# A new order of the work ahead of the steady loop in a metaformer kernel on one core

## Chip, core and metric

The kernel runs on one core of one Trainium2 chip. The metric is device time in microseconds of one execution, taken as the median of several runs. The engines are named as in the profile: PE is TensorE, DVE is VectorE, ACT is ScalarE, POOL is GpSimd, and SP is SyncE, which here only issues DMAs. An SBUF tensor is one in the on-chip working memory; PSUM is the memory that PE writes.

## What is computed

The input x has 16 images of 512 channels and 24 x 8 positions. The reference is, cut to its core:

```python
# attention, over xn = (x - mean_c) / sqrt(var_c + 1e-6), statistics over the channels
ca = sigmoid(mlp(mean_hw(xn)) + mlp(max_hw(xn)))     # mlp(v) = relu(v @ fc1_w.T) @ fc2_w.T, 512 -> 64 -> 512
xa = xn * ca
s  = conv7x7(concat(mean_c(xa), max_c(xa)), sa_w)    # two planes to one, padding 3
x  = x + xa * sigmoid(s)
# feed-forward, per token of 512 channels
def bitlinear(v, w):
    rms = rsqrt(max(mean(w * w), 1e-5))
    wq  = clip(round(w * rms), -1, 1) / rms
    sc  = 127 / max(max(abs(v)), 1e-5)
    return (clip(round(v * sc), -128, 127) / sc) @ wq.T
t = tokens(x)                                         # 16 * 192 tokens
t = t + bitlinear(gelu(bitlinear(layernorm(t), w1)), w2)   # w1: 2048 x 512, w2: 512 x 2048
```

So each weight needs the mean of its squares over the whole matrix before any of it can be rounded, and each image needs its channel gate before the convolution, and the convolution before its feed-forward part.

## The kernel before

The 16 images are taken as 8 pairs of 2 images. A pair has 384 tokens, which are 3 tiles of 128. Everything is written by hand: each engine has one list of instructions, and semaphores tie the lists together. The order in the text of an engine's block is the order in which that engine executes; there is no scheduler, and an instruction that waits holds up all that stands behind it on its engine.

A pair goes through these stages. `load_x` brings it in; `turn_x` on PE turns each tile so that tokens lie on the partitions, and `copy_x` on ACT takes it out of PSUM into `xt`. `channel_stats` and `aggregate` (together `stats1`) on DVE make mean and variance, and `normalise1` on POOL makes the normalised rows `v1`, with three small instructions ahead of three large ones. `turn_v1` on PE turns them back in four blocks of 128 channels; for each block DVE takes maxima (`token_max`) and ACT means (`token_mean`). Then `fc1`, `hidden`, `fc2`, `gate_channels` (a tanh), `split_gate` (five small DVE instructions that split the gate into three bfloat16 parts), `turn_ca`, `copy_caT`, `spread_ca`, `scale_channels` (DVE, writes `pv` and the channel maximum), `sum_channels` (ACT), `split_stats`, and `conv` on PE, 42 small matmuls. After `sum_conv`, `gate_tokens` and `token_gate` each tile gets `add_attention`, `centre` (which on the way needs `rs2`, made by `rstd2` on POOL), `round_x` on POOL, `turn_xq`, `copy_xq`, and `ffn_in`: four blocks of four matmuls (L1139), each followed by a GELU on ACT. `hidden_max` and `hidden_scale` on DVE, `round_g` on POOL and `pack_g` on ACT quantise the hidden rows; SP transposes them by DMA, `ffn_out` (L1150) multiplies by w2, `add_ffn` adds the residual, and the result is turned back and stored.

The weights are loaded as four quarters each of 128 x 2048 values (1 MB). `squares` sums the squares of a quarter, on ACT or on DVE (L865); `weight_sum`, `weight_mean` (PE) and `weight_floor` (DVE, L875, writes `w_ms`) lead to `weight_rms` on POOL (L412). Rounding is one multiply-add on a quarter in place: in this kernel DVE does quarters 0 and 2 (L882) and POOL quarters 1 and 3 (L419). `turn_weights` on PE turns them in eight blocks per weight, through the two PSUM banks `ps_t`, and `copy_weights` on ACT (one instruction) or DVE (two) clips them and writes them into `w1T` or `w2T`. The bands are the convolution's matrices: SP loads the taps in eight small DMAs, `make_taps` (DVE), `place_bands` (PE) and `make_bands` (DVE) prepare them.

In the steady loop (`body`, once per pair) the feed-forward part of one pair, the attention part of the second pair after it and the loading of the third overlap. Ahead of the loop stands a prologue that brings pair 0 through attention, tiles 0 and 1 of it through the first half of the feed-forward part, pair 1 through its convolution and pair 2 to its statistics, and that prepares all weights. The change is to the prologue alone.

## Time and profile before

| | us |
|---|---|
| median of 3 runs (321.93 to 323.15) | 323.08 |
| profiled execution, whole | 323.44 |
| profiled execution, span | 321.7 |
| PE busy | 276.9 (86%) |
| DVE busy | 251.6 (78%) |
| ACT busy | 217.7 (68%) |
| POOL busy | 160.9 (50%) |
| HBM read, written | 14.94 MB, 6.29 MB |

Busy times are sums over the span of 321.7 us of one profiled execution; the whole time of that execution is 1.74 us longer. The page cuts the span into 40 slices of 8 us; the prologue is about the first ten of them. Starts are in microseconds from the start of the span. A merged row of a timeline, such as one with x3, covers several instructions of one kind, and its duration is from the first start to the last end.

### The profile page before, as it was taken

Reading aid. Unit: us, or ns where it says so; the run is one execution under the profiler, and the core shown is the slowest. Engines: PE = TensorE matmul, PEld = TensorE weight load, DVE = VectorE, ACT = ScalarE, POOL = GpSimd, SP = SyncE. Lnnn points to the kernel's source line nnn. Section 1 sums busy time; section 2 is a strip of 40 time slices with the busy share of each in tenths; the row PEclk is TensorE's granted clock in tenths of the full one; section 3 lists DMA queues with packets and bytes.
Section 4 is the critical chain, followed back from the end, with each engine's and each line's share of the span. In section 5 each row is a group of like instructions: output and inputs, shape, how many; then the busy total and the mean of one; then the engine's idle time right before and its main releaser. Section 6 shows DMA issues by size and latency. Waiting matters only on the chain.

```text
span 321.7 us, 5840 instructions
## 1 busy us (share of the span) xinstructions
PE 276.9 (86%) x1834; PEld 155.9 (48%) x1834; DVE 251.6 (78%) x590; ACT 217.7 (68%) x442; POOL 160.9 (50%) x256
## 2 busy tenths in 40 slices
PE   2657669596999979997999799979997999999974
PEld 2444644563456445644564456445644453544431
DVE  0757979879698879887988798878897888899510
ACT  2286397568476976697669766876687669677731
POOL 7404355315855475547554755475547553565420
PEclk9999999859699999999999999999999999999999
DMA  5899300002073209320942094219411732063393
GB/s 131 317 387 421 117 1 2 0 0 51 18 166 65 54 15 254 75 50 17 241 89 48 18 238 91 44 25 235 94 36 32 164 68 51 16 163 74 70 218 98
DMA packets 71078, 34.20 MB, mean 106 GB/s; under 512 B 52040, under 2 KB 68424, under 8 KB 70536
## 3 DMA queue, kind: packets, MB, share of 16 engines
q1 hardware_dynamic: 69384, 32.78, 39.6%
q10 hardware_dynamic: 1664, 1.05, 1.2%
q8 instruction: 15, 0.25, 0.3%
q14 instruction: 15, 0.12, 0.1%
HBM read 14.94 MB, written 6.29 MB: 66 GB/s over the span
## 4 chain that ended last, share of the span: by engine, by line
PE 50%; DVE 12%; POOL 12%; ACT 12%; issue 9%; DMA 3%; SPq 1%; ACTq 0%; POOLq 0%; DVEq 0%
PE ps_o L1150 16%; PE ps_h L1139 9%; PE ps_t L1139 8%; POOL w_room L474 4%; POOL v L451 4%; PE front L1072 4%; ACT w_raw L520 3%; ACT junk_p L520 3%; PE front L1062 3%; PE ps_t L1181 2%; PE small L1088 2%; ACT junk L520 2%; DVE w_room L882 2%; POOL rs L445 2%; PE front L1159 1%
## 5 line engine op out<-in xcount | busy, mean ns | idle before, releaser
L1150 PE MATMUL ps_o<-w2T,hq 128*128 128x512 f16 x384 | 92.7, 380 | 1.2 <-DMA hq<-w_raw 1.2
L474 POOL TENSOR_SCALAR w_room<-w_room,q 128x1024 f32<-128x1024 f32 x48 | 59.3, 1247 | 63.8 <-DVE q L849 63.8
L839 DVE TENSOR_REDUCE amax<-w_room 128x1 f32<-128x1024 f32 (+1 forms) x48 | 57.1, 1208 | 2.2 <-ACT w_room L520 2.2
L1139 PE MATMUL ps_h<-w1T,xq 128*128 128x512 f16 x208 | 54.6, 408 | 0.9 <-ACT xq L520 0.9
L1150 PEld LDWEIGHTS ps_o<-w2T,hq 128*128 128x128 f16 x384 | 35.3, 98 | 37.4 <-issue 3.6
L520 ACT ACTIVATE w_raw<-w_room 128x1024 f16<-128x1024 f16 x48 | 49.4, 1049 | 0.6 <-POOL w_room L474 0.6
L520 ACT ACTIVATE w_room<-ps_h,s 128x512 f32<-128x512 f32 x52 | 35.0, 689 | 14.3 <-PE ps_h L1139 13.1
L1139 PE MATMUL ps_t<-w1T,xq 128*128 128x512 f16 x176 | 43.1, 383 | 0.0
L520 ACT ACTIVATE w_room<-ps_t,s 128x512 f32<-128x512 f32 x44 | 30.2, 688 | 8.3 <-PE ps_t L1139 8.3
L520 ACT ACTIVATE junk_m<-front 128x192 bf16<-128x192 f32 x64 | 20.5, 328 | 21.6 <-DVE pooled L754 21.6
L1139 PEld LDWEIGHTS ps_h<-w1T,xq 128*128 128x128 f16 x208 | 19.8, 103 | 24.2 <-issue 4.8
L463 POOL TENSOR_SCALAR cen<-cen,q 128x512 f32<-128x512 f32 x24 | 16.6, 691 | 27.2 <-DVE q L831 27.2
L856 DVE SCALAR_TENSOR_TENSOR res<-ps_o,s,t 128x512 f32<-128x512 f32 x24 | 17.8, 741 | 12.6 <-PE ps_o L1150 12.6
L1072 PE MATMUL front<-id,v 128*128 128x128 f32 x96 | 18.4, 314 | 10.2 <-POOL v L451 7.5
L1139 PEld LDWEIGHTS ps_t<-w1T,xq 128*128 128x128 f16 x176 | 16.9, 99 | 20.7 <-issue 1.3
L1062 PE MATMUL front<-id,x_in 128*128 128x128 f32 x96 | 17.6, 321 | 6.7 <-DMA x_in<-in_x 5.9
L812 DVE SCALAR_TENSOR_TENSOR t<-pv,sg,xt 128x512 f32<-128x512 f32 x24 | 21.2, 885 | 0.3
L1072 PEld LDWEIGHTS front<-id,v 128*128 128x128 f32 x96 | 12.7, 160 | 17.8 <-POOL v L451 9.5
L741 DVE BATCH_NORM_STATS2 st<-xt 128x6 f32<-128x512 f32 x24 | 15.6, 681 | 7.0 <-ACT xt L520 7.0
L451 POOL TENSOR_SCALAR v<-xt,minus_mean,rs 128x512 f32<-128x512 f32 x24 | 19.8, 828 | 1.4
L520 ACT ACTIVATE w_room<-front 128x512 f32<-128x512 f32 x24 | 14.1, 586 | 8.8 <-PE front L1159 8.8
L754 DVE TENSOR_REDUCE pooled<-front 128x2 f32<-128x384 f32 x32 | 17.5, 548 | 2.3 <-PE front L1072 2.1
(125 smaller groups left out, 459.3 us busy)
## 6 DMA issues: line engine op xcount, KB each, us to landing
out<-w_room SPq DMA_DIRECT2D x16, 384.0 KB, 3.2
x_in<-in_x SPq DMA_DIRECT2D x14, 384.0 KB, 5.1
w_room<-in_L_ffn_w SPq DMA_DIRECT2D x4, 1024.0 KB, 9.1
w_raw<-in_L_ffn_w SPq DMA_DIRECT2D x4, 1024.0 KB, 12.3
x_in<-in_x ACTq DMA_DIRECT2D x2, 384.0 KB, 3.9
hq<-w_raw SPq DMA_TRANSPOSE x48, 3.2
fc_raw<-in_L_conv_fc_w ACTq DMA_DIRECT2D x2, 128.0 KB, 4.3
taps_rev<-in_L_conv_sa_w SPq DMA_DIRECT2D x2, 0.2 KB
```

Of the source, the lines that this page charges most:

```text
L451: pool.tensor_scalar(v1[:, s, :], xt[pair.par][:, s, :], minus_mean[:, s:s + 1], rs1[:, s:s + 1], ALU.add, ALU.mult).then_inc(normed, 1)
L463: pool.tensor_scalar(c[:, :], c[:, :], q1[tile.par][:, 0:1], MAGIC, ALU.mult, ALU.add).then_inc(cen_rounded, 1)
L474: pool.tensor_scalar(part, part, q2[tile.par][:, 0:1], MAGIC, ALU.mult, ALU.add).then_inc(g_rounded, 1)
L520: act.activation(out_ap, in_ap, func, **more).then_inc(signal, 1)
L754: dve.tensor_reduce(pooled[:, k, 0:2], front[bank][:, 0:TOK].rearrange("p (i t) -> p i t", i=2), AX.X, ALU.max).then_inc(max_ready, 1)
L812: link(dve.scalar_tensor_tensor(t_tile, pv[par][:, s, :], sg[par][:, s:s + 1], xt[par][:, s, :], ALU.mult, ALU.add))
L839: chain.mark(dve.tensor_reduce(amax2[:, i:i + 1], w1_room[:, first + i * F // 2:first + (i + 1) * F // 2 + i], AX.X, ALU.max, apply_absolu ...
L856: dve.scalar_tensor_tensor(res[tile.par][:, :], ps_o[:, :], s2[tile.third][:, 0:1], t[tile.pair.par][:, tile.s, :], ALU.mult, ALU.add).the ...
L1062: last = pe.transpose(front[bank][:, tile_cols(k)], x_in[tile.pair.par][:, k, tile_cols(tile.s)], id32[:, :])
L1072: last = pe.transpose(front[bank][:, tile_cols(s)], v1[:, s, tile_cols(k)], id32[:, :])
L1139: last = pe.matmul(banks[b], xq[tile.pair.par][:, tile.s, k, :], w1T[:, k, b * 512:(b + 1) * 512], start=(k == 0), stop=(k == NC - 1))
L1150: last = pe.matmul(ps_o[:, :], hq[tile.par][:, k, :], w2T[:, k, :], start=(k == 0), stop=(k == NF - 1))
```

## The change

The instructions that the steady loop issues stay as they are. Ahead of it, five things are written anew.

SP issues the four DMAs of w1 before it waits for the taps' buffer and before the eight tap DMAs, and loads pair 1 between the second and the third quarter of w2 instead of ahead of w2. POOL alone rounds both weights, quarters 0 to 3 of w1 in a row, and of w2 one quarter after tile 0, one after tile 1, two after pair 1's `normalise1`; DVE keeps only the reciprocals (`weight_unit`). Squares are taken differently: DVE does quarters 0 and 1 of both weights, ACT quarters 2 and 3. DVE copies one more block of w1 (block 5). The third part of the bands goes through PSUM bank `ps_t0` rather than `small`, and PE waits for `band_ready` before the first block of w1. And the lists of all four compute engines bring tile 0, then tile 1, of pair 0 into the feed-forward part before pair 1 gets its statistics and its maxima, where before the two were interleaved.

The core of the diff follows. From ACT's list on, and for DVE's and PE's lists, only the new order is shown, and a + marks a line that stands elsewhere or not at all in before.

```diff
-                    small[:, 256:256 + (BAND_ROWS - 2 * PER_BANK) * ROW_COLS])]
+                    ps_t[0][:, :].bitcast(f32)[:, 0:(BAND_ROWS - 2 * PER_BANK) * ROW_COLS])]
...
-        SQUARES_BY_VECTOR = [(2,), (2, 3)]
-        BY_VECTOR = [(1, 3), (1, 5)]
+        SQUARES_BY_SCALAR = (2, 3)
+        BY_VECTOR = [(1, 3, 5), (1, 5)]
...
+            w1_v = w1.rearrange("(k p) c -> p k c", p=P)
+            w2_v = w2.rearrange("(k p) f -> p k f", p=P)
+            for i in range(4):
+                sp.dma_start(w1_raw[:, 4 * i:4 * i + 4, :], w1_v[:, 4 * i:4 * i + 4, :]).then_inc(w1_loaded[i], 16)
...
             for i in range(4):
-                sp.dma_start(w1_raw[:, 4 * i:4 * i + 4, :], w1_v[:, 4 * i:4 * i + 4, :]).then_inc(w1_loaded[i], 16)
-            load_x(Pair(1))
-            for i in range(4):
+                if i == 2:
+                    load_x(Pair(1))
                 sp.dma_start(w2_raw[:, i, :], w2_v[:, i, :]).then_inc(w2_loaded[i], 16)
             load_x(Pair(2))
...
+            def round_weights(k, raw, quarters):
 
                 pool.wait_ge(w_rms_ready, k + 1)
-                for i in (1, 3):
+                for i in quarters:
                     part = quarter(k, raw, i)
-                    pool.tensor_scalar(part, part, w_rms[:, k:k + 1], MAGIC, ALU.mult, ALU.add).then_inc(w_odd_rounded, 1)
+                    pool.tensor_scalar(part, part, w_rms[:, k:k + 1], MAGIC, ALU.mult, ALU.add).then_inc(w_rounded, 1)
...
             weight_rms(0)
-            round_weights(0, w1_raw)
-            normalise1(Pair(1), 0, 1, 2)
+            round_weights(0, w1_raw, (0, 1, 2, 3))
             rstd2(Tile(Pair(0), 0))
             round_x(Tile(Pair(0), 0))
             weight_rms(1)
-            round_weights(1, w2_raw)
+            round_weights(1, w2_raw, (0,))
             rstd2(Tile(Pair(0), 1))
             round_x(Tile(Pair(0), 1))
+            round_weights(1, w2_raw, (1,))
+            normalise1(Pair(1), 0, 1, 2)
+            round_weights(1, w2_raw, (2, 3))
             round_g(Tile(Pair(0), 0))
             rstd2(Tile(Pair(0), 2))
             round_x(Tile(Pair(0), 2))
...
+            squares(0, w1_raw, w1_loaded, 2)
             for k in range(NC):
                 token_mean(pair0, k, k % 2)
+            squares(0, w1_raw, w1_loaded, 3)
             gate_channels(pair0)
             copy_caT(pair0)
+            squares(1, w2_raw, w2_loaded, 2)
             for s in range(NT):
                 sum_channels(Tile(pair0, s))
+            act.wait_ge(masks_ready, 2)
+            copy_weights(0, (0,))
+            copy_x(Tile(pair1, 0), 1)
+            copy_x(Tile(pair1, 1), 0)
+            copy_weights(0, (2,))
+            gate_tokens(pair0)
+            copy_x(Tile(pair1, 2), 1)
+            squares(1, w2_raw, w2_loaded, 3)
+            copy_weights(0, (4,))
+            copy_xq(Tile(pair0, 0), 0)
+            copy_weights(0, (6, 7))
+            gelu(Tile(pair0, 0), None, h_start)
+            copy_weights(1, (0,))
+            copy_xq(Tile(pair0, 1), 0)
+            gelu(Tile(pair0, 1), None, h_start, (0, 1))
+            copy_weights(1, (2,))
+            gelu(Tile(pair0, 1), None, h_start, (2, 3))
+            token_mean(pair1, 0, 1)
+            copy_weights(1, (3,))
+            token_mean(pair1, 1, 0)
+            copy_weights(1, (4,))
+            token_mean(pair1, 2, 1)
+            copy_xq(Tile(pair0, 2), 0)
+            token_mean(pair1, 3, 1)
+            copy_weights(1, (6, 7))
+            pack_g(Tile(pair0, 0))
+            gate_channels(pair1)
+            copy_x(Tile(pair2, 0), 0)
+            copy_x(Tile(pair2, 1), 1)
+            copy_caT(pair1)
             for s in range(NT):
+                sum_channels(Tile(pair1, s))
             copy_x(Tile(pair2, 2), 0)
...
-            def round_weights(k, raw):
+            def weight_unit(k):
 
                 dve.wait_ge(w_rms_ready, k + 1)
-                for i in (0, 2):
-                    part = quarter(k, raw, i)
-                    dve.tensor_scalar(part, part, w_rms[:, k:k + 1], MAGIC, ALU.mult, ALU.add).then_inc(w_even_rounded, 1)
                 if k == 1:
...
             stats1(pair0, 0, 1, 2)
+            squares(0, w1_raw, w1_loaded, (0, 1))
+            token_max(pair0, 0, 0)
+            token_max(pair0, 1, 1)
             make_taps()
+            token_max(pair0, 2, 0)
+            token_max(pair0, 3, 1)
+            hidden(pair0)
+            weight_sum(0)
             make_bands()
+            weight_floor(0)
             split_gate(pair0)
+            squares(1, w2_raw, w2_loaded, (0,))
+            for s in range(NT):
+                scale_channels(Tile(pair0, s), s % 2)
+            weight_unit(0)
+            copy_weights(0, (1,))
             split_stats(pair0)
+            squares(1, w2_raw, w2_loaded, (1,))
             sum_conv(pair0)
             copy_weights(0, (3,))
             token_gate(pair0)
             add_attention(Tile(pair0, 0))
+            weight_sum(1)
             centre(Tile(pair0, 0))
             weight_floor(1)
+            copy_weights(0, (5,))
             add_attention(Tile(pair0, 1))
+            centre(Tile(pair0, 1))
+            weight_unit(1)
+            stats1(pair1, 0, 1, 2)
             dve.wait_ge(w_turned, 8)
             for i in range(2):
                 dve.memset(g_eps[i], EPS).then_inc(eps_ready, 1)
+            hidden_max(Tile(pair0, 0), 0)
+            copy_weights(1, (1,))
+            hidden_max(Tile(pair0, 0), 1)
+            hidden_scale(Tile(pair0, 0))
+            add_attention(Tile(pair0, 2))
+            token_max(pair1, 0, 1)
+            centre(Tile(pair0, 2))
+            token_max(pair1, 1, 0)
+            hidden_max(Tile(pair0, 1), 0)
+            token_max(pair1, 2, 1)
+            hidden_max(Tile(pair0, 1), 1)
+            hidden_scale(Tile(pair0, 1))
+            copy_weights(1, (5,))
             token_max(pair1, 3, 1)
             hidden(pair1)
             split_gate(pair1)
+            channel_stats(pair2, 0, 1)
+            for s in range(NT):
+                scale_channels(Tile(pair1, s), (1, 0, 1)[s])
             split_stats(pair1)
+            channel_stats(pair2, 2)
             sum_conv(pair1)
             aggregate(pair2, 0, 1, 2)
...
+            a = turn_v1(pair0, 0, 0, a)
             b = turn_v1(pair0, 1, 1, b)
             a = turn_v1(pair0, 2, 0, a)
             b = turn_v1(pair0, 3, 1, b)
+            place_bands()
             fc1(pair0)
             fc2(pair0)
+            weight_mean(0)
             turn_ca(pair0)
             a = spread_ca(Tile(pair0, 0), 0, a)
             b = spread_ca(Tile(pair0, 1), 1, b)
+            pe.wait_ge(band_ready, 2)
+            turn_weights(0, w1_raw, (0,))
             a = spread_ca(Tile(pair0, 2), 0, a)
+            turn_weights(0, w1_raw, (1,))
             b = turn_x(Tile(pair1, 0), 1, b)
             a = turn_x(Tile(pair1, 1), 0, a)
+            conv(pair0)
+            turn_weights(0, w1_raw, (2, 3))
             b = turn_x(Tile(pair1, 2), 1, b)
+            turn_weights(0, w1_raw, (4, 5))
+            weight_mean(1)
+            a = turn_xq(Tile(pair0, 0), 0, a)
+            turn_weights(0, w1_raw, (6, 7))
             weights_ready(0)
+            ffn_in(Tile(pair0, 0), h_start)
+            turn_weights(1, w2_raw, (0, 1))
+            a = turn_xq(Tile(pair0, 1), 0, a)
+            ffn_in(Tile(pair0, 1), h_start, (0, 1))
+            turn_weights(1, w2_raw, (2,))
+            ffn_in(Tile(pair0, 1), h_start, (2, 3))
             b = turn_v1(pair1, 0, 1, b)
+            turn_weights(1, w2_raw, (3,))
+            a = turn_v1(pair1, 1, 0, a)
+            turn_weights(1, w2_raw, (4,))
+            b = turn_v1(pair1, 2, 1, b)
+            turn_weights(1, w2_raw, (5,))
+            a = turn_xq(Tile(pair0, 2), 0, a)
             b = turn_v1(pair1, 3, 1, b)
+            turn_weights(1, w2_raw, (6, 7))
             fc1(pair1)
+            a = turn_x(Tile(pair2, 0), 0, a)
             fc2(pair1)
+            b = turn_x(Tile(pair2, 1), 1, b)
             turn_ca(pair1)
+            weights_ready(1)
             b = spread_ca(Tile(pair1, 0), 1, b)
             a = spread_ca(Tile(pair1, 1), 0, a)
             b = spread_ca(Tile(pair1, 2), 1, b)
             a = turn_x(Tile(pair2, 2), 0, a)
             conv(pair1)
```

On DVE, behind the statistics of pair 0, before had the taps and bands in front of the first maximum (`pooled`):

```order
L747 BN_AGGR mv1<-st1 128x2 x3
L904 COPY taps<-taps_rev 56x2 x8
L906 CAST taps_split<-taps 56x16
L907 TENSOR_TENSOR taps_r1<-taps,taps_split 56x16
L908 CAST taps_split<-taps_r1 56x16
L909 TENSOR_TENSOR taps_split<-taps_r1,taps_split 56x16
L920 CAST band<-ps_h0 128x6x80
L920 CAST band<-ps_h1 128x6x80
L920 CAST band<-small 128x6x16
L923 COPY band_mid<-band 64x6x64 x2
L754 TENSOR_REDUCE pooled<-front0 128x2
```

and now it has (`junk_v,w_sq` is a square of a quarter):

```order
L749 BN_AGGR mv1<-st1 128x2 x3
L867 ISA junk_v,w_sq<-w1_room 128x2048
L867 ISA w_sq 128x1
L867 ISA junk_v,w_sq<-w1_room 128x2048
L867 ISA w_sq 128x1
L756 TENSOR_REDUCE pooled<-front0 128x2
L756 TENSOR_REDUCE pooled<-front1 128x2
L903 COPY taps<-taps_rev 56x2 x8
```

Two squares (L867) took the place of taps and bands; these moved behind the second maximum and behind the sum of the squares.

On POOL, from pair 0's normalised rows (`v`) on, the list was:

```order
L451 TENSOR_SCALAR v<-xt,minus_mean,rs 128x512 x3
L412 TENSOR_TENSOR w_rms<-w_ms,half_pow 128x1
L419 TENSOR_SCALAR w_room<-w_room,w_rms 128x2048 x2
L444 TENSOR_SCALAR ve<-mv 128x3
L445 TENSOR_TENSOR rs<-ve,half_pow 128x3
L446 TENSOR_SCALAR minus_mean<-mv 128x3
L451 TENSOR_SCALAR v<-xt,minus_mean,rs 128x512 x3
```

and now pair 1's normalised rows stand behind all of w1 and two quarters of w2. The list, with the difference marked, from there on:

```order
-L419 TENSOR_SCALAR w_room<-w_room,w_rms 128x2048 x2
+L419 TENSOR_SCALAR w_room<-w_room,w_rms 128x2048 x4
+L438 TENSOR_SCALAR ve<-mv_0 128x1
+L439 TENSOR_TENSOR rs_0<-ve,half_pow 128x1
+L463 TENSOR_SCALAR cen<-cen,q_0 128x512
+L467 TENSOR_SCALAR s_0<-lim,w_unit 128x1
+L412 TENSOR_TENSOR w_rms<-w_ms,half_pow 128x1
+L419 TENSOR_SCALAR w_raw<-w_raw,w_rms 128x2048
+L438 TENSOR_SCALAR ve<-mv_1 128x1
+L439 TENSOR_TENSOR rs_1<-ve,half_pow 128x1
+L463 TENSOR_SCALAR cen<-cen,q_1 128x512
+L467 TENSOR_SCALAR s_0<-lim,w_unit 128x1
```

Four quarters, tile 0, a quarter and tile 1 moved in front of pair 1.

## Rows read from the trace of the kernel before

**Rows 1.** The page, parts 1 and 2: busy time by engine; granted clock in 40 slices.
```profile
PE 276.9 (86%) x1834; PEld 155.9 (48%) x1834; DVE 251.6 (78%) x590; ACT 217.7 (68%) x442; POOL 160.9 (50%) x256
...
PEclk9999999859699999999999999999999999999999
```

**Rows 2.** Timeline of PE: start us, us, engine, line, operation [idle before].
```profile
47.19 1.89 PE L1139 MATMUL ps_h<-w1T,xq 128*128 128x512 f16 x4 [0.87 <-ACT xq L520]
...
81.64 3.57 PE L1139 MATMUL ps_h<-w1T,xq 128*128 128x512 f16 x8
...
114.60 1.89 PE L1139 MATMUL ps_h<-w1T,xq 128*128 128x512 f16 x8
...
146.88 1.89 PE L1139 MATMUL ps_h<-w1T,xq 128*128 128x512 f16 x8
```

**Rows 3.** Timelines of DVE and POOL: floor of w1, normalised rows of pair 1.
```profile
27.88 0.16 DVE L875 TENSOR_SCALAR w_ms<-ps_o 128x1 f32<-128x1 f32 x1 [0.25 <-PE ps_o L1168]
...
40.41 2.79 POOL L451 TENSOR_SCALAR v<-xt,minus_mean,rs 128x512 f32<-128x512 f32 x3
```

**Rows 4.** Timeline of the SP queue; 3:4 us of the windows, GB/s last.
```profile
0.92 6.50 SPq L345 DMA_DIRECT2D taps_rev<-in_L_conv_sa_w  x8
7.46 2.42 SPq L350 DMA_DIRECT2D w_room<-in_L_ffn_w  x4
...
3.00:4.00 1.00, 0.00 (x0) 0.00 (x0) 0.00 (x0) 0.98 (x1) 1.00 (x5) 1.00 1.08 363
```

**Rows 5.** Timelines of PE, DVE, POOL: from x to the first maximum.
```profile
5.85 2.95 PE L1062 MATMUL front<-id,x_in 128*128 128x128 f32 x12 [5.85 <-DMA x_in<-in_x]
...
10.20 0.31 DVE L747 BATCH_NORM_AGGREGATE mv<-st 128x2 f32<-128x6 f32 x3
...
15.34 1.20 DVE L754 TENSOR_REDUCE pooled<-front 128x2 f32<-128x384 f32 x2
...
12.08 2.26 POOL L451 TENSOR_SCALAR v<-xt,minus_mean,rs 128x512 f32<-128x512 f32 x3
```

**Rows 6.** Timeline of DVE: one square of a quarter.
```profile
21.12 2.27 DVE L865 CUSTOM_DVE_ANT_0 junk_v<-w_room 128x2048 bf16<-128x2048 f32 x1
```

**Rows 7.** Lines L419, L882: ns min/median/max, first and last start; timelines, POOL, DVE.
```profile
L419 POOL TENSOR_SCALAR w_room<-w_room,w_rms x2: 1967/2450/2934, 28.8 to 30.7; 128x2048 f32<-128x2048 f32 x2
...
L882 DVE TENSOR_SCALAR w_room<-w_room,w_rms x2: 2598/2798/2998, 29.2 to 31.7; 128x2048 f32<-128x2048 f32 x2
...
28.77 4.88 POOL L419 TENSOR_SCALAR w_room<-w_room,w_rms 128x2048 f32<-128x2048 f32 x2
...
29.22 5.52 DVE L882 TENSOR_SCALAR w_room<-w_room,w_rms 128x2048 f32<-128x2048 f32 x2
```

**Rows 8.** Line L812, then timelines of DVE and POOL: addition beside the rounding.
```profile
L812 DVE SCALAR_TENSOR_TENSOR t<-pv,sg,xt x24: 741/752/2382, 40.1 to 291.5; 128x512 f32<-128x512 f32 x24
...
56.76 2.38 DVE L812 SCALAR_TENSOR_TENSOR t<-pv,sg,xt 128x512 f32<-128x512 f32 x1
...
52.63 5.98 POOL L419 TENSOR_SCALAR w_raw<-w_raw,w_rms 128x2048 f32<-128x2048 f32 x2
```

**Rows 9.** Timelines of DVE and POOL: a small scaling beside GpSimd.
```profile
276.42 0.60 DVE L803 TENSOR_SCALAR sg<-sg_tanh 128x3 f32<-128x3 f32 x1
...
274.78 2.21 POOL L474 TENSOR_SCALAR w_room<-w_room,q 128x1024 f32<-128x1024 f32 x2 [5.19 <-DVE q L849]
```

**Rows 10.** Timelines of ACT, PE, DVE: square, weight copy, packing, transposes, hidden maxima.
```profile
44.66 1.90 ACT L520 ACTIVATE junk<-w_raw 128x2048 bf16<-128x2048 f32 x1
...
68.43 1.11 ACT L520 ACTIVATE w2T<-ps_t,sharp_bias 128x1024 f16<-128x1024 f16 x1 [0.38 <-PE ps_t L1181]
...
76.02 1.99 ACT L520 ACTIVATE w_raw<-w_room 128x1024 f16<-128x1024 f16 x2
...
41.59 2.02 PE L1181 MATMUL ps_t<-id,w_room 128*128 128x128 f16 x16 [0.40 <-ACT w1T L520]
...
77.40 2.34 DVE L839 TENSOR_REDUCE amax<-w_room 128x1 f32<-128x1024 f32 x2
```

More of the change, by code:

```diff
@@ L286, in copied @@
                 if n in banks[k]:
-                    return semaphore, k * len(banks[0]) + banks[k].index(n) + 1
+                    return semaphore, sum(len(banks[j]) for j in range(k)) + banks[k].index(n) + 1
         def wait(eng, semaphore, value):
@@ L595, in copy_out, with squares @@
                      front[bank][:, :].rearrange("p (k q) -> p k q", k=NC), out_ready)
-            def squares(k, raw, loaded, turns):
-                for turn in turns:
-                    i = [i for i in range(4) if i not in SQUARES_BY_VECTOR[k]][turn]
+            def squares(k, raw, loaded, i):
+                for turn in (SQUARES_BY_SCALAR.index(i),):
                     act.wait_ge(loaded[i], 16)
-                    wait(act, squares_done, 3 * k + turn)
+                    wait(act, squares_done, 2 * k + turn)
                     dst = junk[:, :].rearrange("p (a b) -> p a b", b=C) if k == 0 else junk[:, :]
@@ L857, in add_ffn, with squares @@
                                          t[tile.pair.par][:, tile.s, :], ALU.mult, ALU.add).then_inc(res_ready, 1)
-            def squares(k, raw, loaded):
-                for i in SQUARES_BY_VECTOR[k]:
+            def squares(k, raw, loaded, quarters):
+                for i in quarters:
                     dve.wait_ge(loaded[i], 16)
@@ L1264, in _ @@
-            weights_ready(1)
-            b = turn_x(Tile(pair2, 0), 1, b)
-            a = turn_xq(Tile(pair0, 2), 0, a)
-            b = turn_x(Tile(pair2, 1), 1, b)
             a = turn_x(Tile(pair2, 2), 0, a)
```

101 lines of the change are left out of this document (3 added, 98 removed).

## Prediction

> **What bounds the kernel now.** I read the page first: PE is busy for 86% of the span, at the full granted clock (2.4 GHz) except in slices eight to eleven (0.8, 0.5, 0.9, 0.6) [rows 1]. So TensorE bounds the steady loop, and anything that is won ahead of it is won whole. Next the timeline of PE, for the points where stages begin: the loop's first hidden-layer matmul is at 81.64, the second pass at 114.60, the third at 146.88 [rows 2]. A steady pass is 146.88 - 114.60 = 32.28 us, the first one 32.96. The change leaves the loop's code alone, so it can move the time in two places: the start of the loop (81.64), and the 0.68 us by which the first pass is longer.
>
> The start has landmarks. The weight mean square of w1 is floored at 27.88 (call it F) and the normalised rows of pair 1 are finished at 40.41 + 2.79 = 43.20 [rows 3]; tile 0 enters the FFN at 47.19 [rows 2]. After F that is +15.3, +19.3 and, for the loop, +53.8. I rebuild these for the new order, step by step, from durations; "+x" is time after the F of the kernel spoken of. Steps without a row of their own are short ones (each 1.5 us or less) that the new order leaves as they are, with the lengths that the timelines of before give them.
>
> **1. The first load (SyncE queue).** In before, ScalarE issues x as its first work, and SyncE spends 0.92 to 7.42 on eight tap loads before w1 at 7.46; x moves at 363 GB/s with the engines to itself [rows 4] and PE starts at 5.85 [rows 5]. Now w1 is issued at about 0.9, beside x. x is 0.79 MB and needs some 2.2 us at that rate; sharing bytes evenly doubles this, so x lands 2 us later. Bounds: 0 if x goes first; 5 if the engines alternate piece by piece, since contiguous pieces of x are 768 B (192 values) and of w1 2048 B (512 values) (share of x 27%: 0.79 MB in 7.7 us). I take 2.0, the even share of the rate in the row. All later loads come 5 to 6 us earlier, and no row shows a weight being waited for, so that gain is worth nothing by itself.
> The Trainium skill (DMA: Bandwidth & Descriptors, Queues, rings and completion order) says that each DMA engine takes turns between its queue rows packet by packet. It speaks against the move; by it the delay would lie between my 2 and my 5, and the sum does not use it.
>
> **2. Squares in front of the first token maximum (VectorE).** Before, statistics end at 10.20 + 0.31, GpSimd normalises until 12.08 + 2.26 = 14.34, the first maximum starts at 15.34 [rows 5]: 9.6 us after x. Now VectorE squares two quarters of w1 there, 2.27 us each [rows 6]. If GpSimd could run beside them they would end at about the same time as before's maximum (10.5 + 4.7 = 15.2) and cost nothing. But the rows on the rounding show the two engines taking turns. GpSimd's first quarter took 1.97 alone (28.77 to 30.74); VectorE's, issued at 29.22, took 2.60, that is until 1.1 after GpSimd was done; GpSimd's second took 2.93, VectorE's second 3.00 [rows 7]. So a GpSimd quarter costs 1.97 and VectorE's 1.1, one after the other. An addition with three SBUF operands, 0.75 in the median, took 2.38 when GpSimd was in a quarter of w2 that ended at 58.61 [rows 8]; and a scaling of 3 columns took 0.60, until the two GpSimd instructions of 274.78 were done [rows 9]. A square reads SBUF twice too, so the first holds up GpSimd's first small instruction, and the second its next. Delay of the normalised rows: 2 x 2.27 less 0.1 = 4.4. Bounds: 0 and 4.5; I take 4.4, by the nearest rows [rows 7, 8].
> The Trainium skill (SBUF — State Buffer, Who interferes with whom) has the same lock, and names a VectorE instruction with two SBUF inputs beside a reading GpSimd one as a case; the traces agree for the addition (2.38 against 0.75), and nothing here shows it for a square. By it this step costs 4.4, without it 0.
>
> First maximum: 15.34 + 2.0 + 4.4 = 21.7 (before 15.34).
>
> **3. From the first maximum to F.** Before 27.88 - 15.34 = 12.5. Now the weight mean follows fc2 at once. Two maxima 1.15, taps 1.45, two more 1.2, means and fc1 1.8, hidden 0.3, last square of ScalarE and sum 0.8 (ScalarE's means end 4.4 after the first maximum, its square takes 1.90 and the sum's read-out 0.2 [rows 10]), bands 2.3: 9.0. So F = 30.7, against 27.88. The load that comes earlier is overtaken by the wait of step 2.
>
> **4. F to tile 0 in the FFN.** GpSimd starts quarter 0 at +0.9, as before (28.77 - 27.88). In before two engines had all four by 34.7 = +6.9 [rows 7]. Now GpSimd needs 4 x 1.97 = 7.9, and VectorE cuts in: the last step of the gate's split waits for quarter 0 (+3.1, before an own 1.1), then quarter 1 to +5.0, a square of w2 2.3 to +7.3, quarter 2 to +9.2, quarter 3 to +11.1. Behind the square stand three scalings, 2.1, to +9.4; unit and first weight copy, half of it waiting for quarter 3, to +11.5; split of statistics 0.9, convolution 1.3: +13.7. PE turns two blocks of w1 and a tile of x, 2.7, to +16.4 (16 transposes 2.02 [rows 10]); gate, attention and statistics of tile 0 to +18.6; centring waits for ScalarE's square of w2 (+17.0 + 2.1), to +21.2. GpSimd rounds x (0.7), PE turns it and the last two blocks, waiting for the copy that VectorE does behind the floor: +24.5; ScalarE copies, 1.1 each [rows 10]: **+25.9**, before +19.3. On the clock 56.6, before 47.19.
>
> **5. Tile 0 and 1 to pair 1.** GpSimd rounds one quarter of w2 to +25.4, then rstd and x of tile 1 to +28.4, another quarter to +30.4, and only then normalises pair 1, 1.3 of small instructions and 2.8 [rows 3]: **+34.5**, before +15.3. Tile 0 has its GELU done at +30.3 and tile 1 at +37.4, long ahead of the loop, as the order has it. But the loop also needs pair 1.
>
> **6. Pair 1 to the loop.** PE turns its first block at +37.5, behind tile 1; maximum +38.1. VectorE then stands in the centring of tile 2. It needs a GpSimd result queued behind two quarters of w2 (to +38.9, with the addition 0.5 between them), rounding of tile 0's hidden rows, 2.21 [rows 9], and rstd: +42.8; the scale is out at +43.5. Behind it: three maxima 0.6 each, two maxima of hidden rows 1.2 each [rows 10] with their scale 0.4, weight copy 1.1: +49.2. ScalarE: mean 0.7, two weight copies 2.2, then the packing of tile 0, 1.99 [rows 10], which stands ahead of the gate: +54.3 with the tanh. (Before, this packing is at 76.02 = +48.1, so it isn't even early.) Split 1.1, turn, copy and spread 2.4, scalings 2.1, sum 0.8, split 0.8, convolution 1.1: **+62.6**, before +53.8.
>
> **Sum.** 30.7 + 62.6 = 93.3, against 81.64: 11.7 later. The first pass can give back 0.7 (its 32.96 becomes 32.28). Nothing more: GpSimd's normalising of pair 2 still waits for VectorE after the convolution. The profiled execution took 323.44 (span 321.7, 1.7 around it), 0.4 over the median 323.08 of the runs shown. 323.44 + 11.7 - 0.7 = **334.4**. Its own range, 329 to 339: x 5 late adds 3; small instructions that slip between GpSimd's take off up to 5.
>
> **Rivals.**
> A. Squares don't hold GpSimd up. For it: no row shows a square beside GpSimd. Against: the additions. Step 2 loses 4.4, steps 4 to 6 about 2.7 (a square in front of quarters 2 and 3, small waits behind them): 327.3.
> B. Faster. One mechanism: the mean square of w1 comes early enough to carry everything. Its place is the maximum-to-F stretch, 12.5 to 9.0, 3.5 us won. If x isn't late, squares and small instructions wait for nobody, F is 24.3, and the chain from F, GpSimd 0.9 + 7.9, tile 0 +21.6, normalised pair 1 +29.6, convolution +56.2, starts the loop at 80.5: 323.44 - 1.1 - 0.7 = 321.6. It decides from the point where all delays of steps 1 to 6 together stay under 1.8 us. For it: every engine has gaps before 80. Against: rows 7 to 9 each show one of these delays.
> C. The late start is given back. Tiles 0 and 1 arrive packed, so the first passes could run with fewer waits. But PE waits only 1.2 us in a steady pass, so at most some 3 us come back: 331.
> D. The clock. It was at half in slices nine and eleven [rows 1], just before the loop. If the new stretch idles less there, up to 3 us are saved, if more, as much is lost; it doesn't change the order of cases and is in the range.
>
> **Numbers.** Likeliest (all three delays, with C and D inside its range) 0.62; A 0.20; B 0.12; 0.06 for a mix that ends near no change. A measurement of this kernel tells 0.5%, 1.6 us, from no change. B lies just beyond that, so I split it: faster 0.10, same 0.09, slower 0.81. The range that leaves out no more than 2 in 10 takes in A and the likeliest's own: 324.5 to 339.
>
> **What would show it.** Step 1: PE's first transpose at 7 to 8, not 5.9. Step 2: GpSimd's first small instruction of 2.3 us instead of 0.2, first maximum near 21.7. Step 3: floor near 30.7. Step 4: GpSimd's four quarters taking over 9 us, one of them above 4. Step 5: normalised pair 1 near 65. Step 6: a wait of VectorE in the centring of tile 2 of over 2 us, and a loop start near 93. The forecast is wrong if GpSimd's small instructions keep their length beside the squares, or if the loop starts before 85.

## The result and the profile after

The changed kernel took 336.03 us (median; 334.82 to 336.73) against 323.1 us before (321.93 to 323.15): ratio 1.0398, 95% interval [1.0365, 1.043]. The forecast was 334.4, slower, in a range of 324.5 to 339. Direction, size and most of the mechanism held. Two terms of the sum did not, the late start of x and the stretch from F to the loop, and their errors partly cancelled.

The medians differ by 12.9 us, the two profiled executions by 11.4: that of after was the fastest of its four, that of before took a little longer than its median. The traces can account for the 11.4 only.

I read the profiled execution of after (span 333.1 us, 11.4 more than before) by the landmarks of the prediction. First the timeline of PE, which answers to [rows 2] and to PE's row in [rows 5] (start in us, duration in us, engine, line, operation [idle before <-releaser]):

```profile
12.04 2.95 PE L1064 MATMUL front<-id,x_in 128*128 128x128 f32 x12 [12.04 <-DMA x_in<-in_x]
...
58.53 1.86 PE L1141 MATMUL ps_h<-w1T,xq 128*128 128x512 f16 x4 [1.40 <-issue]
...
70.79 0.49 PE L1074 MATMUL front<-id,v 128*128 128x128 f32 x3
...
94.26 3.26 PE L1141 MATMUL ps_h<-w1T,xq 128*128 128x512 f16 x8
...
126.09 1.89 PE L1141 MATMUL ps_h<-w1T,xq 128*128 128x512 f16 x8
...
158.36 1.89 PE L1141 MATMUL ps_h<-w1T,xq 128*128 128x512 f16 x8
```

The loop starts at 94.26 instead of 81.64: 12.62 later. Its first pass is 126.09 - 94.26 = 31.83 against 32.96, which gives back 1.13; the second is 32.27, before 32.28. 12.62 - 1.13 = 11.5, the whole difference of the spans (11.4). Behind the loop's first pass nothing has changed.

The timeline of DVE in after, against the rows of DVE in [rows 3, 5 and 6]:

```profile
16.39 0.31 DVE L749 BATCH_NORM_AGGREGATE mv<-st 128x2 f32<-128x6 f32 x3
16.62 2.26 DVE L867 CUSTOM_DVE_ANT_0 junk_v<-w_room 128x2048 bf16<-128x2048 f32 x1
...
18.92 2.29 DVE L867 CUSTOM_DVE_ANT_0 junk_v<-w_room 128x2048 bf16<-128x2048 f32 x1
...
25.56 1.12 DVE L756 TENSOR_REDUCE pooled<-front 128x2 f32<-128x384 f32 x2 [4.34 <-PE front L1074]
...
34.15 0.16 DVE L877 TENSOR_SCALAR w_ms<-ps_o 128x1 f32<-128x1 f32 x1
...
34.96 0.18 DVE L773 CAST ca_split<-ca_r 128x8 bf16<-128x8 f32 x1
35.17 1.85 DVE L774 TENSOR_TENSOR ca_split<-ca_r,ca_split 128x8 bf16<-128x8 f32 x1
36.95 2.28 DVE L867 CUSTOM_DVE_ANT_0 junk_v<-w_raw 128x2048 bf16<-128x2048 f32 x1
...
74.83 0.21 DVE L830 TENSOR_SCALAR lim<-amax,rs 128x1 f32<-128x1 f32 x1 [1.52 <-POOL rs L439]
```

And GpSimd's, against [rows 3, 7]:

```profile
16.80 2.13 POOL L444 TENSOR_SCALAR ve<-mv 128x3 f32<-128x3 f32 x1 [10.14 <-DVE mv L749]
19.01 2.93 POOL L445 TENSOR_TENSOR rs<-ve,half_pow 128x3 f32<-128x3 f32 x1
...
22.23 2.26 POOL L451 TENSOR_SCALAR v<-xt,minus_mean,rs 128x512 f32<-128x512 f32 x3
...
35.04 10.09 POOL L419 TENSOR_SCALAR w_room<-w_room,w_rms 128x2048 f32<-128x2048 f32 x4
...
64.45 2.26 POOL L451 TENSOR_SCALAR v<-xt,minus_mean,rs 128x512 f32<-128x512 f32 x3
66.69 4.52 POOL L419 TENSOR_SCALAR w_raw<-w_raw,w_rms 128x2048 f32<-128x2048 f32 x2
71.19 2.38 POOL L474 TENSOR_SCALAR w_room<-w_room,q 128x1024 f32<-128x1024 f32 x2
```

In before the first two of these were short (timeline of POOL):

```profile
10.61 0.23 POOL L444 TENSOR_SCALAR ve<-mv 128x3 f32<-128x3 f32 x1 [3.95 <-DVE mv L747]
10.92 0.87 POOL L445 TENSOR_TENSOR rs<-ve,half_pow 128x3 f32<-128x3 f32 x1
```

What the reader is to see: in after the two small GpSimd instructions at 16.80 and 19.01 end about when VectorE's two squares end (18.88 and 21.21), for work that took 0.23 and 0.87 us in before. DVE then stands idle for 4.34 us until PE has turned what GpSimd normalised. At 35.17 it is the other way round: an 8-column operation lasts 1.85 us, until GpSimd's first quarter is done (35.04 and 1.97 more). Below, "the hold" is this: one of the two engines waits until an instruction of the other has ended.

The landmarks against the prediction (start of the loop's first pass last; "+" is time after F, the floor of w1's mean square):

| landmark | before | predicted | after |
|---|---|---|---|
| PE's first transpose (x landed) | 5.85 | 7.9 | 12.04 |
| first token maximum | 15.34 | 21.7 | 25.56 |
| F | 27.88 | 30.7 | 34.15 |
| tile 0 in the FFN | +19.3 | +25.9 | +24.4 |
| pair 1 normalised | +15.3 | +34.5 | +32.6 |
| loop starts | +53.8 | +62.6 | +60.1 |

The first load, in the queue of SyncE and in the windows from 2 us on (DMA share and GB/s last), against [rows 4]:

```profile
0.92 3.63 SPq L341 DMA_DIRECT2D w_room<-in_L_ffn_w  x4
4.59 8.73 SPq L348 DMA_DIRECT2D taps_rev<-in_L_conv_sa_w  x8
...
2.00:3.00 1.00, 0.00 (x0) 0.00 (x0) 0.00 (x0) 0.00 (x0) 0.76 (x5) 1.00 0.83 210
3.00:4.00 1.00, 0.00 (x0) 0.00 (x0) 0.00 (x0) 0.41 (x1) 1.00 (x5) 1.00 0.98 253
4.00:5.00 1.00, 0.00 (x0) 0.00 (x0) 0.00 (x0) 0.88 (x1) 1.00 (x2) 1.00 0.97 341
5.00:6.00 1.00, 0.00 (x0) 0.00 (x0) 0.00 (x0) 0.00 (x0) 1.00 (x2) 1.00 1.03 372
...
8.00:9.00 1.00, 0.00 (x0) 0.00 (x0) 0.00 (x0) 0.00 (x0) 0.00 (x0) 1.00 1.06 392
```

The page of after has `x_in<-in_x ACTq DMA_DIRECT2D x2, 384.0 KB, 8.5`, median time from issue to landing; before it was 3.9.

### The profile page after: what moved, and what is told of

Same layout as the page of the kernel before. It is cut to its first block, busy times and chain, and to the rows that moved or that the text cites. A ratio compares the mean times of both kernels' runs of the same rounds, so it can differ in the third digit from the quotient of the medians.

```text
span 333.1 us, 5836 instructions
## 1 busy us (share of the span) xinstructions
PE 272.0 (82%) x1834; PEld 154.3 (46%) x1834; DVE 250.1 (75%) x590; ACT 214.4 (64%) x439; POOL 172.3 (52%) x260
## 4 chain that ended last, share of the span: by engine, by line
PE 47%; POOL 15%; DVE 12%; ACT 11%; issue 8%; DMA 4%; SPq 1%; ACTq 0%; POOLq 0%; DVEq 0%
PE ps_o L1152 14%; PE ps_h L1141 9%; PE ps_t L1141 8%; ACT w_raw L522 4%; POOL w_room L474 4%; POOL v L451 4%; ACT junk_p L522 3%; DMA x_in<-in_x 3%; PE front L1064 3%; PE front L1074 3%; POOL rs L445 2%; PE small L1090 2%; POOL w_raw L419 2%; POOL ve L444 2%; PE front L1161 1%
## 5 line engine op out<-in xcount | busy, mean ns | idle before, releaser
L1141 PE MATMUL ps_h<-w1T,xq 128*128 128x512 f16 x208 | 52.4, 398 | 3.0 <-issue 1.4
L522 ACT ACTIVATE w_room<-ps_h,s 128x512 f32<-128x512 f32 x52 | 34.9, 688 | 14.2 <-PE ps_h L1141 12.9
L1074 PE MATMUL front<-id,v 128*128 128x128 f32 x96 | 17.6, 302 | 16.2 <-POOL v L451 13.6
L1064 PE MATMUL front<-id,x_in 128*128 128x128 f32 x96 | 18.5, 333 | 12.1 <-DMA x_in<-in_x 12.0
L444 POOL TENSOR_SCALAR ve<-mv 128x1 f32<-128x1 f32 (+2 forms) x13 | 6.2, 474 | 37.9 <-DVE mv L749 37.4
L1064 PEld LDWEIGHTS front<-id,x_in 128*128 128x128 f32 x96 | 13.9, 171 | 14.9 <-issue 12.8
L814 DVE SCALAR_TENSOR_TENSOR t<-pv,sg,xt 128x512 f32<-128x512 f32 x24 | 20.3, 845 | 0.3
## 6 DMA issues: line engine op xcount, KB each, us to landing
out<-w_room SPq DMA_DIRECT2D x16, 384.0 KB, 3.2
x_in<-in_x SPq DMA_DIRECT2D x14, 384.0 KB, 5.0
x_in<-in_x ACTq DMA_DIRECT2D x2, 384.0 KB, 8.5
```

The costliest lines, as they stand in the source:

```text
L522: act.activation(out_ap, in_ap, func, **more).then_inc(signal, 1)
L814: link(dve.scalar_tensor_tensor(t_tile, pv[par][:, s, :], sg[par][:, s:s + 1], xt[par][:, s, :], ALU.mult, ALU.add))
L1064: last = pe.transpose(front[bank][:, tile_cols(k)], x_in[tile.pair.par][:, k, tile_cols(tile.s)], id32[:, :])
L1074: last = pe.transpose(front[bank][:, tile_cols(s)], v1[:, s, tile_cols(k)], id32[:, :])
L1141: last = pe.matmul(banks[b], xq[tile.pair.par][:, tile.s, k, :], w1T[:, k, b * 512:(b + 1) * 512], start=(k == 0), stop=(k == NC - 1))
```

## Experiments

Three theories stood after the result. **Sum**: the loss has separate parts (x late, GpSimd held by squares, GpSimd late for what it has queued), each of which comes back whole when it is undone. **Front only**: the late start of x carries it all. **Tile order**: tile 0 ahead of pair 1 carries it. The runs are in the order in which they were made. Each was timed beside the kernel before, whose median was 322.96 for the first four runs, 322.42 for the next four and 322.66 for the last three. A ratio is that of a run's time to the kernel before, with its 95% interval.

### x_alone: the weight waits until x has landed

```diff
+            sp.wait_ge(x_loaded[0], 32)
             for i in range(4):
                 sp.dma_start(w1_raw[:, 4 * i:4 * i + 4, :], ...
```

> The changed kernel with one wait more: SyncE issues the first weight's load only when both halves of pair 0 have landed, so that x has the DMA engines to itself; the taps still follow. My theory (the new order's first stage is late because x shares the engines with w1): TensorE's first transpose comes back from 12.0 to about 5.9, everything behind it moves along, the floor of w1 from 34.2 to about 28, the loop from 94.3 to about 88, the time from 336.0 to about 330. Rival (the weights' arrival takes its place, since they now come 5 us later): VectorE waits for its quarters, and less than 3 us are won, 333 or more.

Measured 329.95, ratio 1.022 [1.0187, 1.0254]: 6.1 us back. PE starts at 5.64, the loop at 88.46. The load order costs 6.1 us, nearly half of the loss, and "front only" in the narrow sense falls: 7 us remain. DVE's squares now wait for the weight (0.96 and 0.47 us), but the first maximum still comes 13.5 us after x (19.09 - 5.64), as in after. So the earlier issue of the weight was worth nothing.

### read_once_w1 and read_once_all: the squares of VectorE read their tile once

```diff
-  dve.tensor_tensor_reduce(out=dst, in0=part, in1=part, ...)
+  dve.tensor_reduce(w_sq[:, k, i:i + 1], part, ..., ALU.add)
```

The first does it for w1's two quarters, the second for w2's too. These kernels leave out the squaring, and with it the write of the squared rows.

> The changed kernel, but VectorE's two passes over w1 are plain sums, which read SBUF once, and not sums of squares, which read it twice; they are as long. The rounded weights are therefore wrong, and only the time counts. My theory (a square, because it reads twice, locks GpSimd out): GpSimd's small instructions ahead of the normalising of pair 0 shrink from 2.1 and 2.9 to 0.2 and 0.9, the first maximum comes 4.0 earlier, the time is 332. Rival (GpSimd is slowed by something else, such as the loads then under way): no change, 336.

> As before, with the two passes of VectorE over w2 made plain sums too (weights wrong, time counts). My theory: besides the 4.0 us on w1, GpSimd's second quarter of w1 isn't held up for 2.3 us, so it is done with w1 by 39 to 41 in place of 45, and the statistics' split behind scale_channels no longer waits 1.6 for it: about 330. Rival (the delay of GpSimd in its rounding isn't on the path): the same as with w1 alone, 332.

Measured 331.96, ratio 1.0281 [1.0247, 1.0315], and 329.25, ratio 1.0186 [1.0154, 1.0218]. Timeline of POOL in read_once_all:

```profile
17.02 0.19 POOL L444 TENSOR_SCALAR ve<-mv 128x3 f32<-128x3 f32 x1 [10.35 <-DVE mv L749]
17.30 0.88 POOL L445 TENSOR_TENSOR rs<-ve,half_pow 128x3 f32<-128x3 f32 x1
...
31.28 7.82 POOL L419 TENSOR_SCALAR w_room<-w_room,w_rms 128x2048 f32<-128x2048 f32 x4
```

VectorE is as busy as in after (its two sums take 4.58 us together, the two squares 4.59), but the small instructions last 0.19 and 0.88 and the four quarters 7.82 instead of 10.09. So it is not VectorE's time that GpSimd waits for. The sum differs from the square in two things, the second read of SBUF and the write of the result. The write alone doesn't hold GpSimd, as the timeline of DVE in after shows:

```profile
39.27 0.69 DVE L781 CUSTOM_DVE_ANT_0 pv<-v,front 128x512 f32<-128x512 f32 x1
```

This scaling reads `v` from SBUF and `front` from PSUM and writes `pv` to SBUF. It and its two fellows run beside GpSimd's quarters, and all the time that the quarters lost (10.09 - 7.82 = 2.27) is the one square at 36.95. What is left is the second read. This agrees with the Trainium skill (SBUF — State Buffer, Who interferes with whom), which names VectorE instructions with two SBUF inputs. The hold costs 4.1 us ahead of the first maximum and 2.7 us behind the floor. Two SBUF inputs aren't the only case, though: see the run before_pool_alone.

### rstd_first: GpSimd takes the statistics of tile 2 ahead of the rounding of tile 0's hidden rows

```diff
-            round_g(Tile(Pair(0), 0))
             rstd2(Tile(Pair(0), 2))
+            round_g(Tile(Pair(0), 0))
```

> The changed kernel, with GpSimd's rstd of tile 2 ahead of the rounding of tile 0's hidden rows instead of behind it. My theory (VectorE stands in the centring of tile 2 and with it all that pair 1 needs): its wait of 1.5 us goes, the loop starts 1.5 earlier, the time is 334.5. Rival (pair 1 is bound by TensorE's turns and by ScalarE at that point): no change, 336.

Measured 333.6, ratio 1.0332 [1.0301, 1.0363]: 2.4 us back, 1.5 expected, a surplus within the two intervals. The wait is gone, and in its trace the loop starts at 91.73, 2.5 us earlier, of which 0.6 is x: PE starts at 11.40, though nothing in the edit bears on that. The span is only 1.5 us shorter than that of after. So the step is worth 1 to 2 us, in line with the 1.52 us that DVE waited at 74.83.

### before_w1_first: before, with only w1's load ahead of the taps

```diff
+            for i in range(4):
+                sp.dma_start(w1_raw[:, 4 * i:4 * i + 4, :], ...
             for wi in range(W):   # the taps
                 ...
-            for i in range(4):
-                sp.dma_start(w1_raw[:, 4 * i:4 * i + 4, :], ...
```

> The kernel before, with the first part of the change alone: SyncE issues w1 ahead of the taps, and so beside x. My theory: x lands at about 12.0 in place of 5.9 and nothing in the old order hides that, since the weight isn't waited for before; the taps, which VectorE needs ahead of the first maximum there, come at most 1 later than it asks. Everything moves by 6.2: 329 to 330. Rival (the first stage is late, but the squares of w1 follow at once and give it back): 325 or less.

Measured 332.72, ratio 1.0321 [1.03, 1.0343]. This missed by 3 us. PE started at 11.84, as the theory had it; the timeline of DVE shows what it had forgotten:

```profile
19.44 1.17 DVE L904 COPY taps<-taps_rev 56x2 f32<-56x2 f32 x8 [2.94 <-DMA taps_rev<-in_L_conv_sa_w]
...
24.89 1.02 DVE L754 TENSOR_REDUCE pooled<-front 128x2 f32<-128x384 f32 x2
```

The taps, eight loads of under 1 KB each, used to be in DVE's hands at 10.43; issued behind 4 MB of weight they reach it at 19.4, and here DVE takes them in front of its first maximum. Another wait of 2.9 us has taken its place in the queue. After escapes it, since its squares fill that time and its taps stand behind the second maximum.

### before_pool_alone: before, with GpSimd rounding all four quarters

```diff
-                for i in (1, 3):
+                for i in range(4):       # GpSimd
...
-                for i in (0, 2):         # VectorE
-                    dve.tensor_scalar(part, part, w_rms[:, k:k + 1], MAGIC, ...)
```

> The kernel before, with the second part of the change alone: GpSimd rounds all quarters of both weights, VectorE none, in the old order. My theory (the rounding itself isn't what made the new order slow; VectorE gets rid of 5.5 and 4.2 us that it mostly spends waiting for GpSimd): VectorE's split of statistics comes 2 to 3 earlier than 34.9, the last quarter 1.7 later than 34.7; together between no change and 2 us faster, 321 to 323. Rival (GpSimd alone is the price, four quarters at 1.97 on the path): 325 to 327.

Measured 322.14, ratio 0.9986 [0.9969, 1.0003]. GpSimd alone costs nothing that can be measured, in the old order: the two engines took turns anyway [rows 7], and GpSimd has all four quarters done at 28.69 + 7.82 = 36.51, 1.8 us later than the pair of them. VectorE's split of statistics did not come earlier, as the theory had it, but ended at 36.5 instead of 35.7, since each of its steps stood beside a quarter; timeline of DVE:

```profile
30.72 1.90 DVE L790 TENSOR_TENSOR stat_r<-ch_stat,stat_split 128x6 f32<-128x6 f32 x1
32.65 1.94 DVE L791 CAST stat_split<-stat_r 128x6 bf16<-128x6 f32 x1
```

The second is a cast of 6 columns with one SBUF input, which takes 0.18 us in before (35.32). It was held for the rest of GpSimd's quarter like its neighbour with two inputs.

### early_start: before with w1 behind x but ahead of the taps, ACT's squares first, gate's split ahead of the floor

```diff
+            sp.wait_ge(x_loaded[0], 32)
+            (w1's four loads, then the taps)
...
+            squares(0, w1_raw, w1_loaded, (0, 1))   # ACT, ahead of the means
...
-            make_bands()                            # DVE, ahead of the maxima
...
+            squares(0, w1_raw, w1_loaded, (3,))     # DVE, behind the last maximum
             hidden(pair0)
+            make_bands()
+            split_gate(pair0)
```

> The kernel before, with what was good in the new start and without its costs: w1 is issued ahead of the taps, but only once x has landed; ScalarE squares quarters 0 and 1 of w1 while it waits for the first maximum, quarter 2 behind the means; VectorE squares quarter 3 behind the last maximum, while GpSimd has nothing to do; taps behind the second maximum, bands behind the sum; weight mean right behind fc2; the gate is split ahead of the floor. Everything after it is in the old order. My theory: GpSimd starts rounding w1 at 26 in place of 28.8, the split of statistics comes 2.5 earlier, and the loop starts at about 79: 320.5, faster than both. Rival (what comes behind, pair 1 and w2, sets the loop's start anyway): 323.

Measured 324.52, ratio 1.0073 [1.0054, 1.0092]: a miss by 4.0 us, and slower than before. Timeline of DVE:

```profile
15.32 1.20 DVE L755 TENSOR_REDUCE pooled<-front 128x2 f32<-128x384 f32 x2 [4.80 <-PE front L1075]
20.62 0.65 DVE L905 COPY taps<-taps_rev 56x2 f32<-56x2 f32 x8 [4.10 <-DMA taps_rev<-in_L_conv_sa_w]
...
29.10 0.15 DVE L876 TENSOR_SCALAR w_ms<-ps_o 128x1 f32<-128x1 f32 x1
```

The first maximum is in its old place; then DVE waits 4.10 us for taps.

### new_order_freed: after with x alone, ACT's squares first, split ahead of the floor and rstd first

```diff
+            sp.wait_ge(x_loaded[0], 32)
...
-            squares(0, w1_raw, w1_loaded, (0, 1))   # DVE, ahead of the first maximum
...
-            weight_floor(0)
             split_gate(pair0)
+            weight_floor(0)
```

> The changed kernel, with all named costs taken out at once, and its order of tiles and pairs kept, and GpSimd alone rounding: x lands alone, w1's squares are placed as in the run early_start (none while GpSimd normalises), the gate is split ahead of the floor, and the rstd of tile 2 is ahead of the hidden rows' rounding. My theory: these four make up the 13 us, the sum of their single prices is 6.1 + 4.0 + about 1.5 + 1.9 = 13.5: 322.5, the time of the kernel before. Rival (putting tile 0 ahead of pair 1 costs by itself): 326 or more.

Measured 327.93, ratio 1.017 [1.0149, 1.0191]: a miss by 5.4 us. DVE waited 4.08 us for the taps at 20.45, as in early_start. And moving the split ahead of the floor put a square right behind it; timeline of POOL:

```profile
29.16 2.52 POOL L413 TENSOR_TENSOR w_rms<-w_ms,half_pow 128x1 f32<-128x1 f32 x1 [14.98 <-DVE w_ms L879]
31.79 5.86 POOL L420 TENSOR_SCALAR w_room<-w_room,w_rms 128x2048 f32<-128x2048 f32 x3
```

The power took 2.52 instead of 0.55 (after, 34.40): the edit that freed DVE from GpSimd handed the hold to GpSimd, one step earlier on the chain. So this kernel isn't free of all named costs, and its miss doesn't yet speak for the rival.

### taps_back_first, early_start_taps_first, new_order_taps_first: the taps ahead of w1 again

```diff
-            (wait for x and w1's four loads ahead of the taps)
+            (w1's four loads behind the taps)
```

applied to after (which has no wait for x), to early_start and to new_order_freed.

> After with only the order of the loads put back: taps ahead of the first weight, which then is issued at about 7.46 as before. Theory (the loss is three parts: x late, GpSimd locked out by DVE's two squares ahead of the first maximum, and tile 0 ahead of pair 1): x is back at about 5.9, the lockout of 4 us stays, and DVE's squares can wait for the weight up to 2 us longer than in x_alone (329.95), where it was issued at 5.5. So 330 to 332, I say 331. Rival (the whole loss is the load order): 323 to 325.

> early_start with the taps ahead of the first weight, as before. Theory: the 4.1 us that DVE waited for taps behind the weight were the miss of early_start, and nothing else stands in their place but the weight, about 2 us later: the floor at about 26 (before 27.88, early_start 29.10) and 320.5 to 322, I say 321.2. Rival (ACT's early squares, which now wait for the weight, push the means and with them the later maxima): 323 to 325.

> new_order_freed (the new tile order, squares placed early on ACT) with the taps ahead of the first weight. Theory: the wait of 4.1 us for taps goes as in early_start_taps_first, the lockout of GpSimd's pow by the square of w2 (2 us) and the order of tile 0 stay: 324 to 325.5, I say 324.8. Rival (tile 0 ahead of pair 1 costs by itself as much as the front): 327 or more.

Measured 329.81, ratio 1.0239 [1.0179, 1.0298]; 322.57, ratio 0.9998 [0.998, 1.0016]; 326.34, ratio 1.0121 [1.0086, 1.0155]. Putting the loads back gives after 6.2 us (331 was expected), as x_alone did. Three of its four executions took 329.1 to 330.1 us; the profiled one took 333.35, with longer steady passes, but its loop starts at 88.68, as in x_alone (88.46). In early_start the wait for taps is gone, and the time is that of before: 1.4 us over what I expected, because the wait that the rival names was there too. The third is 1.5 us over. Timeline of ACT in early_start_taps_first:

```profile
13.03 1.91 ACT L520 ACTIVATE junk<-w_room 128x2048 bf16<-128x2048 f32 x1 [2.21 <-DMA w_room<-in_L_ffn_w]
15.72 1.91 ACT L520 ACTIVATE junk<-w_room 128x2048 bf16<-128x2048 f32 x1 [0.69 <-DMA w_room<-in_L_ffn_w]
17.63 0.31 ACT L520 ACTIVATE junk_m<-front 128x192 bf16<-128x192 f32 x1
```

The squares wait for the weight, the means for the squares, and PE then waits 2.81 us for a mean at 18.49; the floor came at 27.42, expected at 26. In these kernels early weight and early taps exclude each other on SyncE's queue: whichever is second holds the front up. A load from another engine's queue was not tried.

The pair early_start_taps_first and new_order_taps_first have the same front up to the floor (27.42 and 27.07). Their medians differ by 3.8 us, their profiled executions by 1.6 (spans 321.5 and 323.1; loops at 81.47 and 83.70). But they differ in more than the order of tile 0. First the timeline of POOL in early_start_taps_first, then those of POOL and PE in new_order_taps_first:

```profile
27.65 0.55 POOL L412 TENSOR_TENSOR w_rms<-w_ms,half_pow 128x1 f32<-128x1 f32 x1 [13.57 <-DVE w_ms L875]
...
27.30 2.52 POOL L412 TENSOR_TENSOR w_rms<-w_ms,half_pow 128x1 f32<-128x1 f32 x1 [13.01 <-DVE w_ms L878]
...
32.04 1.01 PE L1184 MATMUL ps_t<-id,w_room 128*128 128x128 f16 x8 [2.53 <-POOL w_room L419]
```

In the second kernel GpSimd's power is still held by the square of w2, for 2.0 us, and PE waits 2.53 us for the quarter that follows it. They also differ in who rounds (priced only in the old order, by before_pool_alone), in the place of pair 1's load and in who takes which square. Counted from the floor, the loop starts 2.6 us later in the second (56.63 for 54.05). If the hold counts in full, 0.6 of that is left, and 1.8 of the medians' 3.8. That is an estimate of what the order of tile 0 costs together with the other differences; no run shows its price alone.

For the 12.6 us by which the loop starts later in after, the landmarks give this account: x 6.2 later; from x to the first maximum 4.0 more, the two squares; from there to F 3.9 less, where the weight mean now follows fc2 at once; from F to the loop 6.3 more, of which read_once_all finds 2.7 and rstd_first some 1.5. The last 2 us are the new order and whatever else lies there. None of the versions beats the kernel before by a measurable amount.

## Why the prediction was right, and where it was not

**Step 1, x: mis-sized.** Taken 2.0, bounds 0 and 5, measured 12.04 - 5.85 = 6.2, and x_alone gives back 6.1. The even share of bytes was the wrong choice, and even the upper bound was short. The DMA view counts packets, MB and busy share of each queue (q1 is SyncE's, here w1; q10 is ScalarE's, here x and behind it the two small matrices `fc1_w` and `fc2_w`). After up to 10 us, then before up to 4.5 us:

```profile
q1 hardware_dynamic: 927, 1.87, 52.6%
q10 hardware_dynamic: 1063, 0.82, 27.9%
...
q10 hardware_dynamic: 1032, 0.78, 58.1%
```

The two queues moved about as many packets, but w1's are 2048 B and x's 768 B, so w1 got more than twice the bytes. The 0.79 MB of x were through at about 9.8 us (0.70 MB of that queue at 9, 0.82 at 10), against 4.5 in before: 5.3 us later. That is what the upper bound stood for; with the prediction's own figures it is 7.7 - 2.2 = 5.5, not 5. The other 0.9 us, between x's last bytes and PE's start, stay open. The Trainium skill (DMA: Bandwidth & Descriptors, Queues, rings and completion order) with its turn per packet pointed this way.

**Step 2, squares and GpSimd: right.** From x to the first maximum it took 25.56 - 12.04 = 13.5 against 15.34 - 5.85 = 9.5 before (the prediction has 9.6): 4.0, taken 4.4. The weight was no longer waited for, as step 3 said. read_once_w1 shows the cause: 4.1 us come back. The argument was weaker than its result: it took the square from the addition because both have two SBUF inputs, while [rows 7, 9] already show VectorE's instructions with one SBUF tensor as input in turns with GpSimd.

**Step 3, maximum to floor: right.** Taken 9.0, measured 34.15 - 25.56 = 8.6, before 12.5.

**Step 4, F to tile 0: over-sized by 1.5.** +25.9 taken, +24.4 measured. GpSimd's quarters were forecast to end at +11.1 and ended at 35.04 + 10.09 = 45.13, +11.0; the last step of the gate's split lasted 1.85, as expected in kind. The 1.5 us too many lie elsewhere: the convolution ended at +12.7, taken +13.7, and the rest is behind it. The cost of the hold there is shown by read_once_all, 2.7 us, the figure that rival A had for steps 4 to 6.

**Step 5, pair 1: over-sized by 1.9, its role wrong.** +34.5 taken, +32.6 measured. PE turns the first block of pair 1 only at 70.79, 4.1 us after GpSimd had it (66.71), since tile 1 stands ahead on PE. So it was the tiles on PE, not the normalising, that set this stage; step 6 did start from PE, so the sum was not hurt.

**Step 6, pair 1 to the loop: over-sized.** From tile 0 in the FFN to the loop 36.7 us were taken and 35.7 measured, so steps 5 and 6 together were 1.0 too long. DVE's wait in the centring of tile 2 was there but 1.52 us, not over 2, since GpSimd's two quarters of w2 ended at +37.1 instead of +38.9; rstd_first gives it back. The packing ahead of the gate did not bind: on ACT it ended at 85.73, and fc2 on PE, which the tanh at 85.79 also needs, at 85.75. Loop at +60.1 for +62.6.

**The sum.** Start of the loop 93.3 taken, 94.26 measured; given back 0.7 taken, 1.1 measured. In the start of the loop, measured less taken, the errors were +4.2 (x), -0.4, -0.4 (steps 2 and 3) and -2.5 (F to loop). That the total came within 1.6 us of the median is partly luck.

**The rivals.** A (squares hold nobody) falls by the row at 16.80 and by both read_once runs. B (faster) needed x on time and no hold. new_order_taps_first has x on time and the two early squares out of the way; its floor comes at 27.07, not at B's 24.3, and its fastest execution, 324.8, is still above the 322.66 of before. One hold of 2.0 us is left in it, so B's case in full was not run. C (given back): 1.1 us of 12.6. (Its 1.2 us of waiting in a steady pass counts one of three waits of PE; they are 1.9 together.) D (clock): the granted clock of after was 0.5 to 0.7 in slices three to twelve except the ninth (0.5 is the lower level, 1.2 GHz), in before only in slices nine and eleven [rows 1]:

```profile
PEclk9965556795569999999999999999999999999999
```

Four runs of after had mean clocks of 0.907 to 0.96 and took 334.8 to 336.7, the lowest clock the shortest time, so it doesn't decide here. What the low clock costs in the front was not measured.

## What to carry to other kernels

A load that is moved to the front is not free because its queue is idle: price what it does to the load that the first engine waits for, and to the small loads that fall behind it. Before a filler is put into an engine's idle time, look at which other engine runs then, and whether the trace shows instructions of the filler's kind in turns with it (here squares, roundings, casts and additions of VectorE with GpSimd, but not plain sums); the idle time was there because the chain ran on that other engine. When the single costs are undone one by one, look in each trace whether another cost has come in its place, before a difference is put down to what is left. And when one wait is taken away, walk the same engine's queue for the next thing that lands late; here it was the taps, three times.
